# Residual combine stage: rolled loop with two buffers replaced by an unrolled one with four, scaling by ScalarE, stores on SyncE

## What is computed

```python
xn = _layernorm(x, axis=-1)          # (x - mean) / sqrt(var + 1e-5)
s = _L0_attn_ref(xn, ...)
g = _silu(_L0_ffn_ref(xn, ...))
x = x + s * g
xn = _layernorm(x, axis=-1)
...
x = x + s * g
return x
```

## Time and profile before

| | us |
|---|---|
| median of 3 runs | 9283.21 |
| the profiled execution, its own time | 9277.52 |
| its span | 9275.7 |
| PE busy | 7053.4 (76%) |
| DVE busy | 6068.0 (65%) |
| ACT busy | 5394.3 (58%) |
| POOL busy | 4177.2 (45%) |

### The profile page before, as it was taken

One profiled execution on the slowest core, in us unless ns is written; L12 is line 12 of the kernel. 1 busy time (PEld: TensorE's weight loads), 2 busy tenths in 40 slices (PEclk: granted clock), 3 DMA queues, 4 the chain that ended last, 5 costly groups with the idle time before them and its releaser, 6 DMA issues. The chain is left out here.

```text
span 9275.7 us, 216671 instructions
## 1 busy us (share of the span) xinstructions
PE 7053.4 (76%) x72180; PEld 4817.1 (52%) x72628; DVE 6068.0 (65%) x12819; ACT 5394.3 (58%) x13666; POOL 4177.2 (45%) x3667
## 2 busy tenths in 40 slices
PE   5767888888888888888888849997888747633357
PEld 2325665665565566565555638886555512222245
DVE  6876776766767677676667736666666668744432
ACT  4446777777777777777777724444666644311112
POOL 4555554555555555555555514444444445521000
PEclk8889999999999999999999969998999978866578
DMA  2320000000000000000000010000000033222000
GB/s 115 122 88 15 10 10 22 12 11 19 13 11 17 15 11 10 22 10 11 20 12 11 17 64 5 5 5 15 16 19 16 14 131 121 106 74 70 19 0 27
DMA packets 166840, 305.70 MB, mean 33 GB/s; under 512 B 23432, under 2 KB 123168, under 8 KB 147744
## 3 DMA queue, kind: packets, MB, share of 16 engines
q1 hardware_dynamic: 140752, 262.32, 8.7%
q10 hardware_dynamic: 18768, 23.20, 0.7%
q0 software_dynamic: 6144, 5.25, 0.4%
HBM read 208.74 MB, written 31.64 MB: 26 GB/s over the span
## 5 line engine op out<-in xcount | busy, mean ns | idle before, releaser
L822 ACT ACTIVATE L0f_scores<-L0f_scores,L0f_nmx,L0f_rn 128x128 f32<-128x128 f32 x3072 | 1339.1, 443 | 86.4 <-DVE L0f_nmx L926 85.3
L1008 PE MATMUL L0f_ring<-L0f_wqkv,L0f_hT 128*128 128x512 f32 x2324 | 1224.0, 633 | 104.9 <-DMA L0f_scales<-L_ffn_scales_dram 59.9
L752 POOL TENSOR_TENSOR L0f_qr<-L0f_qs,L0f_table 128x512 f32<-128x512 f32 x776 | 989.5, 1275 | 547.0 <-ACT L0f_qs L793 480.8
L759 POOL TENSOR_TENSOR L0f_qr<-L0f_qr,L0f_m 128x512 f32<-128x512 f32 x776 | 986.0, 1271 | 278.1 <-issue 131.8
L766 POOL TENSOR_TENSOR L0f_qr<-L0f_qr,L0f_rn 128x512 f32<-128x512 f32 x388 | 396.2, 1042 | 786.5 <-DVE L0f_rn L918 784.9
L924 DVE TENSOR_REDUCE L0f_mx<-L0f_scores 128x8 f32<-128x1024 f32 x384 | 469.4, 1222 | 360.8 <-PE L0f_scores L1036 183.9
L895 DVE TENSOR_TENSOR L0f_m<-L0f_ring,L0f_table 128x512 f32<-128x512 f32 x776 | 522.1, 688 | 262.5 <-ACT L0f_qs L793 241.7
L822 ACT ACTIVATION_READ_ACCUMULATOR L0f_scores<-L0f_scores,L0f_nmx,L0f_rn 128x1 f32 x3072 | 668.5, 218 | 0.0
L837 ACT ACTIVATE L0f_oT<-L0f_o 128x512 f32<-128x512 f32 x385 | 235.4, 611 | 639.5 <-PE L0f_o L1074 597.5
L1008 PEld LDWEIGHTS L0f_ring<-L0f_wqkv,L0f_hT 128*128 128x128 f32 x2324 | 396.9, 197 | 382.1 <-issue 289.9
L1070 PE MATMUL L0f_o<-L0f_pT,L0f_vb 128*64 128x96 f32 (+1 forms) x6160 | 501.7, 280 | 97.3 <-DVE L0f_pT L941 81.5
(11 more groups left out here) (533 smaller groups left out, 19082.7 us busy)
## 6 DMA issues: line engine op xcount, KB each, us to landing
L0a_bc_all<-L0a_bc_rows SPq DMA_DIRECT2D x32, 2048.0 KB, 11.3
L2a_bc_all<-L2a_bc_rows SPq DMA_DIRECT2D x32, 2048.0 KB, 11.3
L0f_vmix<-L0f_vb SPq DMA_DIRECT2D x288, 128.0 KB, 2.3
L1f_vmix<-L1f_vb SPq DMA_DIRECT2D x96, 128.0 KB, 2.3
L0f_wqkv<-L_ffn_wqkv_dram SPq DMA_DIRECT2D x7, 1536.0 KB, 6.0
L2f_parts<-L2f_zero ACTq DMA_DIRECT2D x10, 832.0 KB, 13.8
n_s<-mixer_out SPq DMA_DIRECT2D x32, 256.0 KB, 4.1
L2f_back<-L2f_parts SPq DMA_DIRECT2D x32, 256.0 KB, 4.0
```

Source lines behind the costliest of these rows:

```text
L752: e.tensor_tensor(rotated, qs[:, q % QN], spread(cos, 1, 8), ALU.mult).then_inc(cosed.sem, 1)
L759: e.tensor_tensor(rotated, rotated, m2[:, q % SN], ALU.add).then_inc(added.sem, 1)
L822: a = e.activation(s_ps[:, h, j], s_ps[:, h, j], ACT.Exp, bias=nmx[:, s, col:col + 1], scale=rn[:, tt, 2 * u, col:col + 1], accum_out=sums ...
L1008: e.matmul(bank[:], hT[:, tt * P:tt * P + P], wqkv[:, col:col + 512], start=True, stop=True).then_inc(full, 1)
```

## The change

Every loop of the stage over the batches is unrolled in all programs, so that indices and semaphore values are constants. `xb`, `s` and `xo` have four buffers, `stats`, `mv`, `rstd` and the new `shifted` two. There are 13 semaphores in place of 8, and no credits are handed out. DVE no longer normalises: POOL computes, behind the inverse root, the product with the mean and its negation (`shifted`), and ACT scales the four tiles from `xo` to `g.f` with scale and bias, having issued the silu of batch b+2 before the scaling of batch b. The stores move from ACT's queue to SP's, behind all sixteen (n0: eight) loads of the stage. DVE waits for the store and the scaling of batch b-4 only between its multiplication and its addition, and `added` is signalled by the addition itself rather than by the drain behind it.

```diff
 
 
     with stage(nc, name) as r:
-        xb = r.sb("xb", [P, 2, TT, C])
-        sb_ = r.sb("s", [P, 2, TT, C])
+        NBUF = 4
+        xb = r.sb("xb", [P, NBUF, TT, C])
+        sb_ = r.sb("s", [P, NBUF, TT, C])
         fb = r.sb("fb", [P, 2, TT, C])
-        xo = r.sb("xo", [P, 2, TT, C])
-        stats = r.sb("stats", [P, TT, 6])
-        mv = r.sb("mv", [P, TT, 2])
-        rstd = r.sb("rstd", [P, TT])
+        xo = r.sb("xo", [P, NBUF, TT, C])
+        stats = r.sb("stats", [P, 2, TT, 6])
+        mv = r.sb("mv", [P, 2, TT, 2])
+        rstd = r.sb("rstd", [P, 2, TT])
+        shifted = r.sb("shifted", [P, 2, TT])
         half = r.sb("half", [P, TT])
         eps = r.sb("eps", [P, TT])
-        loaded = [r.sem(f"loaded{k}") for k in range(2)]
-        sent = [r.sem(f"sent{k}") for k in range(2)]
-        silued = r.count("silued", [0, 1])
-        added = r.count("added", [0, 1])
-        measured = r.count("measured", [0, 1])
-        rstd_ready = r.count("rstd_ready", [0, 1])
+        loaded = [r.sem(f"loaded{k}") for k in range(NBUF)]
+        sent = [r.sem(f"sent{k}") for k in range(NBUF)]
+        silued, added, measured = r.sem("silued"), r.sem("added"), r.sem("measured")
+        rstd_ready, normed = r.sem("rstd_ready"), r.sem("normed")
         block = r.block()
         PER = 32 if mixed else 16
-
-        def pairs(e, body):
-
-            with e.Fori(0, BATCH // 2) as h:
-                for k in range(2):
-                    body(h, k, h * 2 + k)
+        view = lambda t, b: t[b:b + 1].rearrange("o (t p) c -> p (o t) c", p=P)
 
         @block.sync
         def _(e):
-            r.give_credit(e)
-            view = lambda t, b: t[bass.ds(b, 1)].rearrange("o (t p) c -> p (o t) c", p=P)
-
-            def load(h, k, b):
-                e.wait_ge(*added(h, k, 2))
+            for b in range(BATCH):
+                k = b % NBUF
+                if b >= NBUF:
+                    e.wait_ge(added, b - NBUF + 1)
                 e.dma_start(xb[:, k], view(x_in, b)).then_inc(loaded[k], 16)
                 if mixed:
                     e.dma_start(sb_[:, k], view(g.s_dram, b)).then_inc(loaded[k], 16)
-            pairs(e, load)
+            if x_out is not None:
+                for b in range(BATCH):
+                    e.wait_ge(added, b + 1)
+                    e.dma_start(view(x_out, b), xo[:, b % NBUF]).then_inc(sent[b % NBUF], 16)
+                for k in range(NBUF):
+                    e.wait_ge(sent[k], 16 * (BATCH // NBUF))
 
         @block.scalar
         def _(e):
-            view = lambda t, b: t[bass.ds(b, 1)].rearrange("o (t p) c -> p (o t) c", p=P)
-            for k in range(2):
-                e.sem_inc(sent[k], 16)
-
-            def body(h, k, b):
-                if mixed:
-                    e.wait_ge(*added(h, k, 2))
-                    e.activation(fb[:, k], g.f[:, bass.ds(b * TT, TT), :], ACT.Silu).then_inc(silued.sem, 1)
-                if x_out is not None:
-                    e.wait_ge(*added(h, k))
-                    e.dma_start(view(x_out, b), xo[:, k]).then_inc(sent[k], 16)
-            if mixed or x_out is not None:
-                pairs(e, body)
-            if x_out is not None:
-                for k in range(2):
-                    e.wait_ge(sent[k], 16 * (BATCH // 2 + 1))
+            def silu(b):
+                if b >= 2:
+                    e.wait_ge(added, b - 1)
+                e.activation(fb[:, b % 2], g.f[:, b * TT:b * TT + TT, :], ACT.Silu).then_inc(silued, 1)
+
+            def norm(b):
+                e.wait_ge(rstd_ready, b + 1)
+                for tt in range(TT):
+                    o = e.activation(g.f[:, b * TT + tt, :], xo[:, b % NBUF, tt], ACT.Identity,
+                                     bias=shifted[:, b % 2, tt:tt + 1], scale=rstd[:, b % 2, tt:tt + 1])
+                o.then_inc(normed, 1)
+
+            if mixed:
+                for b in range(2):
+                    silu(b)
+            for b in range(BATCH):
+                if mixed and b + 2 < BATCH:
+                    silu(b + 2)
+                if again:
+                    norm(b)
 
         @block.gpsimd
         def _(e):
             e.memset(half[:], -0.5)
             e.memset(eps[:], EPS)
             e.drain()
-
-            def body(h, k, b):
-                e.wait_ge(*measured(h, k))
-                e.tensor_tensor(rstd[:], mv[:, :, 1], eps[:], ALU.add)
-                e.drain()
-                e.tensor_tensor(rstd[:], rstd[:], half[:], ALU.pow).then_inc(rstd_ready.sem, 1)
             if again:
-                pairs(e, body)
+                for b in range(BATCH):
+                    k = b % 2
+                    e.wait_ge(measured, b + 1)
+                    if b >= 2:
+                        e.wait_ge(normed, b - 1)
+                    e.tensor_tensor(rstd[:, k], mv[:, k, :, 1], eps[:], ALU.add)
+                    e.drain()
+                    e.tensor_tensor(rstd[:, k], rstd[:, k], half[:], ALU.pow)
+                    e.drain()
+                    e.tensor_tensor(shifted[:, k], rstd[:, k], mv[:, k, :, 0], ALU.mult)
+                    e.drain()
+                    e.tensor_scalar(shifted[:, k], shifted[:, k], -1.0, None, ALU.mult)
+                    e.drain().then_inc(rstd_ready, 1)
 
         @block.vector
         def _(e):
-            def body(h, k, b):
-                e.wait_ge(loaded[k], h * PER + PER)
-                if x_out is not None:
-                    e.wait_ge(sent[k], h * 16 + 16)
+            for b in range(BATCH):
+                k = b % NBUF
+                e.wait_ge(loaded[k], PER * (b // NBUF + 1))
                 if mixed:
-                    e.wait_ge(*silued(h, k))
-                    e.tensor_tensor(sb_[:, k], sb_[:, k], fb[:, k], ALU.mult)
-                    e.drain()
-                    e.tensor_tensor(xo[:, k], sb_[:, k], xb[:, k], ALU.add)
+                    e.wait_ge(silued, b + 1)
+                    e.tensor_tensor(sb_[:, k], sb_[:, k], fb[:, b % 2], ALU.mult)
+                    e.drain()
+                if b >= NBUF:
+                    if x_out is not None:
+                        e.wait_ge(sent[k], 16 * (b // NBUF))
+                    if again:
+                        e.wait_ge(normed, b - NBUF + 1)
+                if mixed:
+                    e.tensor_tensor(xo[:, k], sb_[:, k], xb[:, k], ALU.add).then_inc(added, 1)
                 else:
-                    e.tensor_copy(xo[:, k], xb[:, k])
-                e.drain().then_inc(added.sem, 1)
+                    e.tensor_copy(xo[:, k], xb[:, k]).then_inc(added, 1)
                 if not again:
-                    return
+                    continue
+                e.drain()
+                if b >= 2:
+                    e.wait_ge(rstd_ready, b - 1)
                 for tt in range(TT):
-                    e.bn_stats(stats[:, tt], xo[:, k, tt])
+                    e.bn_stats(stats[:, b % 2, tt], xo[:, k, tt])
                 e.drain()
                 for tt in range(TT):
-                    e.bn_aggr(mv[:, tt], stats[:, tt])
-                e.drain().then_inc(measured.sem, 1)
-                e.wait_ge(*rstd_ready(h, k))
-                for tt in range(TT):
-                    e.tensor_scalar(g.f[:, bass.ds(b * TT + tt, 1), :].rearrange("p o c -> p (o c)"), xo[:, k, tt],
-                                    mv[:, tt, 0:1], rstd[:, tt:tt + 1], ALU.subtract, ALU.mult)
-                e.drain()
-            pairs(e, body)
+                    e.bn_aggr(mv[:, b % 2, tt], stats[:, b % 2, tt])
+                e.drain().then_inc(measured, 1)
 
 
 class Shared:
```

## The result

The changed kernel takes 9134.5 us (median of four, 9123.4 to 9144.9) against 9283.1 before, a ratio of 0.984 (95% interval 0.983 to 0.986): 148.6 us faster, where 73 were forecast and 9195 was the low end of the range. The direction and the price of the stage came out; the other half of the gain was in no term of the sum.

The account below looks back on a forecast made before the run. No engine is full; each batch is a serial DVE, POOL, DVE chain. Savings of 15.9 (n0), 17.3, 16.4, 16.4 and 7.3 (n4) give -73.3 us: 9277.5 to 9204.2, plus 5.7 for the median, 9210; range 9195 to 9229.

Parts of the forecast that it names:

- part 1: Stages with norm: scaling moved to ACT and batches pipelined, DVE's period per batch 3.27 us where 6.32 stood.
- stall: DVE waits for store 0 before the addition of batch 4: 2.0 us once a stage, ends 1.0 and 2.8.
- POOL's pace in n0: In n0, with copy and norm, POOL's 2.4 us a batch binds, not DVE's part.
- the ring of three batches: DVE, POOL, ACT, silu and back to DVE takes 7.85 us against 9.8 for three periods, so doesn't bind.
- part 2: Loads four deep on SP alone: first not delayed, 3.93 us from issue to DVE's start; later batches arrive fast enough.
- part 3: Stores on SP behind all loads: store 0 delays batch 4's addition 2.0 us; in n4 it lands 3.5 after issue.
- A: Stage pipeline costs more than its parts through code fetches, delayed loads, late store 0: +13 us, 9223; chance 0.22.
- B: Stage costs less than counted: early-met waits vanish behind drains, no stall; 9196 to 9203; chance 0.13.
- C: ACT switches tables between silu and Identity, two 1.28 us loads a batch: +42 us in n1 to n3, 9252; chance 0.03.
- E: Batches stay serial because waits on rstd_ready or the scaling are one batch too strict: about 9260; chance 0.03.
- Rival D: Later stages' moved code makes the kernel slower, needing a 92 us loss there; +-7 us at 0.08%; chance 0.02.

## Why the prediction was right in the stage and wrong in the sum

*Period (part 1).* Right in mechanism, 0.2 high: 3.06 instead of 3.27; I had allowed 0.35 a batch for drains and waits, and the rows leave 0.14. Seven periods are 1.5 us less in n1 to n3; the later first load (0.4) and the longer stall (0.3) took back 0.7 of it. POOL's pace in n0 was about 2.5 where 2.4 stood, ACT's 1.65 exact. Two things it did not foresee: POOL's power took 1.32 us beside DVE in n1 (1.01 before), and the addition of batch 6 waited 0.52 us for ACT, so the ring of three batches was nearer to binding than 7.85 against 9.8 said.

*Loads (part 2).* The first was slightly later, 4.3 us to DVE's start instead of 3.93, and the `s` loads landed a median of 5.0 us after issue (4.1 before). It cost nothing more in n1 to n3. In n4 DVE waited 0.91, 0.34, 0.35 and 0.34 us for the loads of batches 1 to 4, for which the sum had no term.

*Stores (part 3).* The stall was 2.32 us for 2.0. In n4 it was mis-sized: 5.14 us, because store 0, issued at 9129.22, let DVE go on 5.1 us later, behind load 7, where I put 3.5. The DVE line of n4's fifth addition:

```profile
9134.32 0.69 DVE L3110 TENSOR_TENSOR n_xo<-n_s,n_xb 128x512 f32<-128x512 f32 x1 [5.14 <-DMA out_dram<-n_xo]
```

With the waits for loads it makes n4 the only stage that gained less than forecast, -6.1 for -7.3. In n4 the last load, issued at 9128.58, took 5.0 us and landed at 9133.6, and store 0 was there 0.7 us behind it; in n1 the last load landed at 5321.8 and store 0 let DVE go on at 5322.55. So in both stages store 0 came 0.7 to 0.8 us behind the last load. Whether it waits for that load no run shows; if it does, which is my estimate from these two, the term that was mis-sized is the landing of load 7, 5.0 us where the earlier trace rows have 3.21.

*Rivals A, B, C, E.* B came nearest for n1 to n3 in the period, though not in the stall. A's sign, DMA ahead of the multiplications of batches 1 to 3, showed in n4 alone. For C, n1 loads a table once, at 5302.99, and Identity and Silu alternate behind it without another. E's sign, DVE idle ahead of the statistics with POOL as releaser, did show in n0, 0.17 to 0.79 us from batch 3 on; but the wait is for the roots of two batches before, as written, and comes because POOL sets the pace there, as forecast. No batch waited for the one before. E's price was off: its own terms, put into the sum, give about 9270, not 9260.

*Rival D is the step that failed.* It put moved code at +-7 us, bounded by "473.5 and 473.9 us between the same two instructions, 0.08%", and weighed anything larger only as a loss; what the code's place did was -61 us in L0f, and 67 us in the medians with and without it (9134.5, 9201.6). The pair, mixers L0a and L2a, was no bound for L0f: 21 or 22 blocks are fetched in L0a in 618 us, after and before, while L0f fetched 444. The profile of before held the warning: 461 and 444 instruction packets in L0f's window (queues 8 and 14), and 85 us of DVE idle time there in six lines under "issue" (37.5, 18.9, 16.2, 8.0, 2.6 and 1.8). And the two signs were not alike. Of eight places tried for DVE's loop in the kernel before (0, 35, 43, 47, 51, 55, 67 and 102), one was slow, 51, the one at which it stood, and all seven others gained. So the second half of the result is luck: the change happened to push the loop off its slow place. Nor was the price of a place what I had in mind, the fetch itself: 45 of 68 us are L926 held by POOL, which the time between two instructions of a mixer without that pair couldn't show.

## What to carry over

Price an edit by its stage, then ask separately what it does to the place of the code behind it: here DVE's loop of 305 instructions in L0f came with 443 or 444 instruction packets of 8.2 KB at six of eight places and with 262 and 258 at the other two, and it cost time at one place alone, 51 (4626.9 us, against 4553.0 to 4568.7 at the other seven), where 0.36 us more of idle time ahead of one L934 made the L926 behind it meet POOL's operation. Compare a suspicious gain with a kernel in which only idle instructions move the code, and read it by stages; here it split 148 us into 75 that belong to the change and some 60 to 70 that idle instructions alone could bring or take. Of n1's 20 us with the stores between the loads, 7.5 are the scaling off DVE and 0.5 the four buffers; the other 12 are the overlap of batches over engines, the unrolling and the stores' new place, which no run took apart. Where a short DVE operation shows a mean several times its shortest (L926: 455 ns, shortest 166), look which operation of POOL it ends with.

## Not expected of the hardware

The same loop brought more or fewer instruction packets of 8.2 KB, according to its place modulo 128 instructions. DVE's of 305 had 443 in L0f's window at 35 and 262 at 0, (443 - 262) / 42 = 4.3 a pass; moving ACT's of 302 by 28 took 443 to 263, as many a pass. The spots 128 apart idled DVE by 0.45 us (the L909 of place 51) or by nothing that shows (place 67), according to the instruction they fell on, and ACT's 180 packets cost nothing measurable (9282.2 us without them, 9283.0 with). A DVE operation of 0.17 us took up to 1.28 us when it began behind POOL's (L926, above), and the place of the code decided whether it did: 0.36 us of lateness cost 1.4 us a pass. SP's issue took longer with loads outstanding; that these are the reason is argued. The first six took 0.40 to 0.51 us each in n1, the seventh twice that (start, duration):

```profile
5305.63 0.51 SPq L3044 DMA_DIRECT2D n_s<-mixer_out  x1
5306.18 1.04 SPq L3042 DMA_DIRECT2D n_xb<-x_dram  x1
```
